# Keys of a decoder's two context attentions made per sequence, with a reordered head and filler matmuls

## What is computed

```
x = x + _L0_attn_ref(_layernorm(x, axis=-1), ...)   # 16 heads of 8, adds its own input
x = x + _L0_xattn_ref(_layernorm(x, axis=-1), ctx_768, ...)   # 8 heads of 64 over the context
x = x + _L0_ffn_ref(_layernorm(x, axis=-1), ...)    # "mixer": 16 heads of 8, tokens in two classes
x = x + _L1_attn_ref(_layernorm(x, axis=-1), ...)   # delta rule, a scan over the tokens
x = x + _L1_xattn_ref(_layernorm(x, axis=-1), ctx_768, ...)   # 16 heads of 64 over the context
x = x + _L1_ffn_ref(_layernorm(x, axis=-1), ...)    # ternary weights, gelu
```

```
k = encoder_hidden_states @ Wk
scores = jnp.einsum('bhsd,bhkd->bhsk', q, k) * scale
```

## Time and profile before

| | |
|---|---|
| median of 3 runs | 436.03 us (434.42 to 437.32) |
| the profiled execution | 432.25 us |
| its span, first to last instruction | 430.5 us |
| granted TensorE clock, mean over the span | 0.988 |
| TensorE busy (matmul) | 358.3 us, 83% |
| VectorE busy | 267.5 us, 62% |
| ScalarE busy | 209.8 us, 49% |
| POOL busy | 120.7 us, 28% |

### The profile page before, as it was taken

The page is one execution under the profiler, slowest core; times in us unless marked ns, Lnnn a source line. Parts: engine busy times, 40 slices in busy tenths (PEclk is TensorE's granted clock), DMA queues, the critical chain, the costliest instruction groups (busy, mean ns, idle before and its releaser), DMA issues. The chain is left out here.

```text
span 430.5 us, 7408 instructions
## 1 busy us (share of the span) xinstructions
PE 358.3 (83%) x2801; PEld 206.1 (48%) x2801; DVE 267.5 (62%) x579; ACT 209.8 (49%) x359; POOL 120.7 (28%) x113
## 2 busy tenths in 40 slices
PE   2677788889888989768799998867978999999986
PEld 1444333345454644335455664533534556555555
DVE  4864654566646566567644677759886675667345
ACT  2354556546434453236566443524645664445534
POOL 4000000136454017000000231114694655356500
PEclk9998999999999999899999998999999999999999
DMA  7700000010000000000001000000000000000000
GB/s 200 204 1 2 0 2 1 2 50 2 0 2 2 0 0 2 0 0 3 3 2 50 0 2 0 2 0 0 2 2 2 2 0 2 2 0 2 2 2 24
DMA packets 9688, 6.16 MB, mean 14 GB/s; under 512 B 3755, under 2 KB 8758, under 8 KB 9654
## 3 DMA queue, kind: packets, MB, share of 16 engines
q1 hardware_dynamic: 9654, 5.69, 5.1%
HBM read 5.39 MB, written 0.26 MB: 13 GB/s over the span
## 5 line engine op out<-in xcount | busy, mean ns | idle before, releaser
L1269 DVE TENSOR_REDUCE mxw<-PS 128x2 f32<-128x1024 f32 x48 | 58.5, 1222 | 23.8 <-PE PS L637 23.4
L1040 ACT ACTIVATE Pc<-PS 128x1024 f32<-128x1024 f32 x48 | 49.1, 1023 | 22.3 <-PE PS L665 21.1
L552 POOL TENSOR_TENSOR Psum<-Pc 128x512 f32<-128x512 f32 x24 | 31.0, 1293 | 100.5 <-ACT Pc L1040 99.8
L1266 DVE TENSOR_REDUCE mx<-PS 128x4 f32<-128x1024 f32 x32 | 39.0, 1223 | 24.2 <-PE PS L630 24.1
L693 PE MATMUL ACC<-Pc,V 128*64 128x256 f32 x384 | 52.0, 391 | 0.0
L554 POOL TENSOR_TENSOR Psum<-Psum,Pc 128x512 f32<-128x512 f32 x22 | 27.9, 1269 | 38.3 <-ACT Pc L1040 38.0
L1040 ACT ACTIVATE Ps<-PS 128x1024 f32<-128x1024 f32 x32 | 32.7, 1023 | 12.0 <-PE PS L649 10.9
L693 PEld LDWEIGHTS ACC<-Pc,V 128*64 128x64 f32 x384 | 23.4, 136 | 23.6 <-issue 15.2
L705 PE MATMUL PS<-ones_h 128*128 128x512 f16 x102 | 25.4, 391 | 4.7 <-DVE small_kv L1318 2.5
L555 POOL TENSOR_TENSOR Psum<-Psum,Pc 128x512 f32<-128x512 f32 x22 | 28.0, 1273 | 1.7
L658 PE MATMUL PS<-Qhl,Khl_a 64*128 64x256 f16 x384 | 26.5, 271 | 0.9 <-DVE scratch L1438 0.5
(11 more groups left out here) (290 smaller groups left out, 701.7 us busy)
## 6 DMA issues: line engine op xcount, KB each, us to landing
Qm<-mrow SPq DMA_DIRECT2D x64, 0.5 KB, 1.7
wq_c<-in_c_Wq_dram SPq DMA_DIRECT2D x1, 512.0 KB, 5.5
spread<-in_c_Wo_dram SPq DMA_DIRECT2D x1, 512.0 KB
Pc<-in_ctx_dram SPq DMA_DIRECT2D x1, 384.0 KB, 4.6
wk_c<-in_c_Wk_dram SPq DMA_DIRECT2D x1, 384.0 KB, 6.7
wv_c<-in_c_Wv_dram SPq DMA_DIRECT2D x1, 384.0 KB, 7.6
csth<-in_const_dram SPq DMA_DIRECT2D x1, 320.0 KB, 4.9
x<-in_x_dram SPq DMA_DIRECT2D x2, 128.0 KB, 2.2
```

The lines of the kernel that those rows point to most:

```text
L552: alone(v.tensor_tensor(t, p[:, :, 0, :], p[:, :, 1, :], ALU.add), "sums_done")
L1040: e = A(to, src.rearrange("p a c -> p (a c)"), ACT.Exp, scale=PHASES[name].scale)
L1266: last = v.tensor_reduce(to, src.rearrange("p e (t s) -> p e t s", t=2), AX, ALU.max)
L1269: last = v.tensor_reduce(to, src, AX, ALU.max)
```

## The change

Four things are done.

1. Keys per sequence: K and K2 exist now for b = 0 and b = 1, each with one f32 matmul of 512 columns, one area, copies of 128x512. The plan places 24 pairs of jobs instead of 12; in the first attentions at steps 2 to 8 and 12 instead of 3, 6, 8 and 12. K moves from the kinds that take two areas to those that take one, which also moves the areas of all jobs behind it until the ring meets again.
2. Head: sequence 1's ln stands behind sequence 0's ln2 and xt.
3. POOL writes ones_h before everything else, and 12 filler matmuls stand ahead of the first transposes.
4. prep does its four matmuls with high halves first and waits for the low half only then.

```diff
-    K0, K1 = ([[job("K", n, 0, u), job("K2", n, 0, u)] for u in range(PHASES[n].U)] for n in (x0, y1))
+    (K0, K0_), (K1, K1_) = ([[[job("K", n, b, u), job("K2", n, b, u)] for u in range(PHASES[n].U)] for b in range(B)]
+                            for n in (x0, y1))
...
-    head = ln + ln_ + ln2 + xt + [job("kq", a0, 0)]
+    head = ln + ln2 + xt + ln_ + [job("kq", a0, 0)]
...
-        3: K0[0], 6: K0[1], 8: K0[2], 10: [zT], 11: [out] + ln + V0[0], 12: ln2 + V0[1] + K0[3], 13: xt + V0[2],
+        2: K0[0], 3: K0_[0], 4: K0[1], 5: K0_[1], 6: K0[2], 7: K0_[2], 8: K0[3], 10: [zT], 11: [out] + ln + V0[0], 12: ln2 + V0[1] + K0_[3], 13: xt + V0[2],
...
-        -8: V1[4], -7: K1[1], -5: K1[2], -3: K1[3], 1: [qx], 3: [rs], 7: [rt], 10: [rv], 11: [zT, qx_], 12: [out, rs_] + ln, 13: ln2 + V1[5], 14: xt,
+        -8: V1[4], -7: K1[1], -6: K1_[1], -5: K1[2], -4: K1_[2], -3: K1[3], -2: K1_[3], 1: [qx], 3: [rs], 7: [rt], 10: [rv], 11: [zT, qx_], 12: [out, rs_] + ln, 13: ln2 + V1[5], 14: xt,
...
-        -8: [dg_], -5: K1[7] + [dt], -4: [s0], -2: [s1], 0: [s2], 2: [s3], 4: [oT], 5: [dl], 6: [dl2],
+        -8: [dg_], -6: K1[7], -5: K1_[7] + [dt], -4: [s0], -2: [s1], 0: [s2], 2: [s3], 4: [oT], 5: [dl], 6: [dl2],
...
 WARM = {
+    job("xt"): 12,
...
-    BANKS = {k: n for n, ks in ((2, ("prep", "M", "S", "ctx", "K", "V", "dp", "dt", "sp")),
-                                (1, ("xt", "kq", "vs", "turn", "Q", "zT", "out", "most", "qt", "simT", "qx", "rs", "rt", "rv", "dg", "oT",
+    BANKS = {k: n for n, ks in ((2, ("prep", "M", "S", "ctx", "V", "dp", "dt", "sp")),
+                                (1, ("xt", "kq", "vs", "turn", "K", "Q", "zT", "out", "most", "qt", "simT", "qx", "rs", "rt", "rv", "dg", "oT",
...
-                    after(sp, "K", "cross0", 0, 3)
+                    for k in range(B):
+                        after(sp, "K", "cross0", k, 3)
...
+            alone(v.memset(ones_h[:], 1.0), "warm_set")
             alone(v.memset(spread[:], 0.0), "pool_set")
...
-            alone(v.memset(ones_h[:], 1.0), "ones_set")
...
-                    after(pe, "kq", name, b)
+                    pe.wait_ge(sem("kq_high"), count("kq", name, b))
...
-                    for X, w in enumerate((spread_k, spread_q)):
-                        for uu in range(2):
-                            to, unit = dst[:, X, uu * S:(uu + 1) * S], slice((2 * u + uu) * P, (2 * u + uu + 1) * P)
-                            mm(to, w["h"][:, unit], hl16[:, b, 0, X * S:(X + 1) * S], start=(uu == 0), stop=False)
-                            last = mm(to, w["l"][:, unit], hl16[:, b, 1, X * S:(X + 1) * S], start=False, stop=not classes and uu == 1)
+                    for part, half in enumerate("hl"):
+                        if half == "l":
+                            after(pe, "kq", name, b)
+                        for X, w in enumerate((spread_k, spread_q)):
+                            for uu in range(2):
+                                to, unit = dst[:, X, uu * S:(uu + 1) * S], slice((2 * u + uu) * P, (2 * u + uu + 1) * P)
+                                last = mm(to, w[half][:, unit], hl16[:, b, part, X * S:(X + 1) * S], start=(part == 0 and uu == 0),
+                                          stop=part == 1 and not classes and uu == 1)
...
-                    for h in range(B):
-                        last = mm(dst[:, h, :], wk2[name][:, u * P:(u + 1) * P], ctxT[:, h * SC:(h + 1) * SC],
-                                  start=True, stop=True)
-                    last.then_inc(sem("ring"), 1)
+                    mm(dst[:, 0, :], wk2[name][:, u * P:(u + 1) * P], ctxT[:, b * SC:(b + 1) * SC],
+                       start=True, stop=True).then_inc(sem("ring"), 1)
...
-                    A(keys(name, 0, u), src.rearrange("p a c -> p (a c)"), ACT.Identity).then_inc(sem("k_high"), 1)
+                    A(keys(name, 0, u)[:, b * SC:(b + 1) * SC], src[:, 0, :], ACT.Identity).then_inc(sem("k_high"), 1)
...
-                    v.tensor_tensor(keys(name, 1, u), src.rearrange("p a c -> p (a c)"), keys(name, 0, u), ALU.subtract)\
+                    t = slice(b * SC, (b + 1) * SC)
+                    v.tensor_tensor(keys(name, 1, u)[:, t], src[:, 0, :], keys(name, 0, u)[:, t], ALU.subtract)\
```

More of the change, by code:

```diff
@@ L189, in schedule @@
     qt, kq, sim, simT, vs = mixer_front(1)[3:]
-    classes = V1[0] + cross_tail(x0, 1) + ln + [job("gsum")] + V1[1] + V1[2] + ln2 + xt + [qt, sim, kq, vs, job("tg")] + K1[0] + [simT, job("cls", f0)] + V1[3] + tern
+    classes = V1[0] + cross_tail(x0, 1) + ln + [job("gsum")] + V1[1] + V1[2] + ln2 + xt + [qt, sim, kq, vs, job("tg")] + K1[0] + K1_[0] + [simT, job("cls", f0)] + V1[3] + tern
     two = attentions((f0, 0, -9, 0), (f0, 1, -4, 0))
@@ L200, in schedule @@
     place_in(two, {
-        -8: V1[4], -7: K1[1], -5: K1[2], -3: K1[3], 1: [qx], 3: [rs], 7: [rt], 10: [rv], 11: [zT, qx_], 12: [out, rs_] + ln, 13: ln2 + V1[5], 14: xt,
+        -8: V1[4], -7: K1[1], -6: K1_[1], -5: K1[2], -4: K1_[2], -3: K1[3], -2: K1_[3], 1: [qx], 3: [rs], 7: [rt], 10: [rv], 11: [zT, qx_], 12: [out, rs_] + ln, 13: ln2 + V1[5], 14: xt,
         15: [dp, rt_], 16: [dn, dn2, dg], 18: [dt]})
-    ends = [rv_, s0] + V1[6] + [zT_, s1, out_] + V1[7] + [s2] + ln_ + [s3] + K1[4] + [oT] + ln2_ + [dl] + xt_ + K1[5][:1] \
-        + [dl2, yT, dp_] + K1[5][1:] + [dout] + ln4 + K1[6][:1] + ln24 + xt4 + [dn_] + K1[6][1:] + [dn2_]
+    ends = [rv_, s0] + V1[6] + [zT_, s1, out_] + V1[7] + [s2] + ln_ + [s3] + K1[4] + K1_[4] + [oT] + ln2_ + [dl] + xt_ + K1[5][:1] + K1_[5][:1] \
+        + [dl2, yT, dp_] + K1[5][1:] + K1_[5][1:] + [dout] + ln4 + K1[6][:1] + K1_[6][:1] + ln24 + xt4 + [dn_] + K1[6][1:] + K1_[6][1:] + [dn2_]
     three = attentions((y1, 0, -9, 0), (y1, 1, 13, 2))
@@ L624, in maxima @@
                         after(pe, "Q", name, b, u // 2)
-                        after(pe, "K", name, 0, u)
+                        after(pe, "K", name, b, u)
                 dst = take(j)
@@ L700, in keep_busy @@
                 if not warm_ready:
-                    pe.wait_ge(sem("ones_set"), 3)
+                    pe.wait_ge(sem("warm_set"), 1)
                     warm_ready.append(True)
@@ L715, in _ @@
                     if j == first_cross_s:
-                        pe.wait_ge(sem("ones_set"), 3)
+                        pe.wait_ge(sem("ones_set"), 2)
                         pe.wait_ge(sem("one_row_set"), 3)
```

## The result

The changed kernel takes 419.62 us (median of 4 runs, 418.54 to 419.66), beside it the kernel before 435.23 (median of 4, 431.81 to 437.32); ratio 0.964, 95% interval 0.958 to 0.971. Forecast were 424.6, between 419 and 432, with a chance of 0.85 for faster by over 1%. The profiled execution takes 419.58 us, span 417.8: 12.7 less than that of before (432.25), where the sum of the prediction had 11.4.

A forecast was written before the change was run, and what follows sets the result against it. TensorE, busy 83% of the span and mostly waiting for PSUM areas, was the bound. 2.8 + 2.6 + 4.2 + 2.2 - 0.4 = 11.4 us off 432.25 left 420.9; plus 3.8, median 424.6, range 419 to 432.

The forecast's parts named there:

- Head: Kernel start up to ScalarE's copy at 13.13 us: earlier rows, full clock and split spreading gain 2.8 us (0.3 to 3.5).
- First attentions: 30 to 75 us: sum of waits stays, clock's 1.6 us and a 0.99 us wait are gained; 2.6 us.
- Mixer's units: 157 to 190 us: waits of 2.45 and 2.01 shrink to 1.2 and 0.8, clock held; 4.2 us (0.5 to 6).
- Delta rule: 255 to 290 us: fillers need only sequence 0's low half, now before the reduction; 2.2 us (1.0 to 2.7).
- Costs: Extra copy time on VectorE and ScalarE, 3.8 us of engine time, charged at 0.4 us, at most 3.8.
- ring of areas: Six areas taken in other positions, 30 to 185 us; TensorE waits there for reductions, not areas: zero, plus or minus 1.5.
- slower: Rival: 16 halves ahead of the delta rule each stall TensorE 1.9 us; with 13 stalls 442.3 us; chance 0.06.
- step to the median: Whole kernel: 3.8 us, old median 436.03 above its profiled execution, added to the predicted 420.9 us.
- waits whole: Rival: each low half queues behind a reduction, so only head and delta rule gain, 5.0 us: 431.0; chance 0.18.
- Clock not held: Rival: pauses behind the head's transposes and keys, and the 1.9 us wait, lower the clock: 427.9 us; chance 0.11.
- Fillers too long: Rival in the head: TensorE starts at 2.2 us, fillers end at 7.3, gain 1.0 less: 425.6; no separate chance.
- signs: Trace marks of being right: copy about 10.3, spreading rows at most 0.3, clock 1.00 at 30-62 us, line 1324 waits at most 2.

The follow-up runs named there:

- head_only: Changed kernel with whole key units in two areas back at their old places, the new head kept; 431.36 us.
- keys_only: Changed kernel with its head put back (old norm order, no 12 fillers, ones and spreading as before), split keys kept; 423.02 us.
- turn_fillers: Changed kernel with 5 more filler matmuls of 512 columns ahead of the second turn of the first attention; 420.48 us.
- low_half_first: Changed kernel with each low half put ahead of the reductions of its step on VectorE; 422.59 us.
- u7_late: Changed kernel with both halves of the last key unit at the place of the whole one; 423.18 us.
- cross0_whole: Changed kernel with the keys of the first cross attention alone whole again, in two areas at their old places; 425.83 us.
- two_areas: Changed kernel, same order on every engine, but each half unit of keys takes two PSUM areas; 439.78 us.
- no_fillers: Changed kernel without the 12 filler matmuls ahead of the first transposes; 420.99 us.

## Why the prediction was right, and where it was not

- Head, 2.8 forecast: 2.98 at ScalarE's copy, 3.1 at the full clock (head_only, keys_only). Start of the fillers 0.98 for 1.2, their end 6.08 for 6.2, spacing 0.43 as read. The normed rows stand at 5.22 + 0.62 = 5.84 for 5.8, so the lower gain of 2.6, reckoned from the Trainium skill's rule on POOL and VectorE (GPSIMD Engine Reference, section 1 Specifications), did not come. The reading behind it was weak: in the trace of before POOL's casts run from 3.65 to 5.14 us, beside the row of 0.17 as well as that of 0.47. By parts: fillers 1.8 (I had 1.25; the spreading's clock was missing), spreading 1.3 by its trace (I had 1.4).
- First attentions, 2.6 forecast: 2.8 in the traces, and by the path I gave: the waits keep their sum and the clock's 1.6 comes back. But the reason given for the clock, that after 1.9 us of waiting it stays, is refuted by turn_fillers. What holds is a frequency: over all executions the three kernels with whole keys in both attentions or with two areas have 0.965 to 0.988, the changed one 0.996 to 1.000. It is no sharp line: low_half_first and u7_late, with split keys in single areas, reach down to 0.984.
- Mixer's units, 4.2 forecast: 4.05 up to 181 us, and 0.7 more by the third turn, where a score matmul waits 0.23 us for ScalarE and not 0.75. The waits came about as laid out (1.2 and 0.8 forecast, 1.05 and 0.62 measured); the first even better than I wrote, for 1.22 + 0.68 - 0.86 is 1.04 and not 1.2. What I had not seen is that they hang on the ring's position, which the first attentions set (cross0_whole).
- Delta rule, 2.2 forecast: 2.3 in the wait (2.54 to 0.20); u7_late returns 1.8 of it in the wait. Another 1.1 us between 250 and 270 was low clock in the trace of before (four key matmuls 3.40 us there, 1.88 after), which my sum did not hold.
- Costs, 0.4: not separately visible. VectorE's busy sum rose by 1.1 us (267.5 to 268.6); no run tells how much of it is on the path.
- What failed in the sum's reasoning is the ring of areas, "zero, plus or minus 1.5", with the reason that TensorE waits there for reductions and not for areas. Two runs bear on it. cross0_whole shows what the position does: 3.9 us at the full clock where the first attentions' own waits were booked at 1.2, and 1.0 of it is one wait for an area that another job asks for. two_areas shows what the size does: 12.4 us at the full clock. My layout had the single areas in it, and so the waits came out right; but I priced as a side effect what the other terms stood on. The rival "slower" did not happen in the changed kernel (three waits over 1.3 us for a low half). In two_areas the kernel is slower than before, though with no wait for a low half over 2.0 us.
- The sum (11.4) was 1.3 short of the difference of the profiled executions (12.7), and that it was not further off is partly luck: 1.1 us that the head lost again at 19 us and 1.1 of low clock that went near the delta rule were both not in it, and cancel.
- The time itself, 424.6 for 419.6, missed by 5.0, and most of that, 3.8, came from the step to the median: I added the distance between before's median and its profiled execution to the changed kernel too. That distance was mostly low clock, of which before has more in many of its executions than in the profiled one (0.969 to 0.988, profiled 0.988). The changed kernel, at 0.996 to 1.000, does not have it.
- Of the rivals: waits whole, refuted (7.8 for 13.2 us). Clock not held: the low clock came, not behind the transposes and keys as the rival had it but at 19 us, and cost 1.1 us in the traced execution; two others have the same mean clock, the fourth has 1.000. Fillers too long, refuted.
- Of the signs, the copy (10.15 for 10.3), the clock from 30 to 62 us, the longest wait (1.74) and the fillers of the delta rule came as said. That no matmul of the spreading takes over 0.3 us holds in the head but not at 19.19 us, where eight take 1.69 us, 0.21 apart instead of 0.11.

## What to carry to other kernels

When jobs share a ring of buffers, count what each takes before counting when it is done: in this order of jobs, halving what the keys take was worth 12 us, and splitting them without that cost more than it gave. A part's price measured alone holds only as long as the ring stands in the same position behind it, so undo parts both singly and together. And before a profiled time is carried over to a median, look at the granted clock of all executions: a difference that is low clock in the one kernel need not be there in the other.

## What the runs showed of the chip that I had not expected

In these traces the granted clock falls behind pauses of 1.05 to 2.5 us (in cross0_whole once behind one of 0.65), but not behind the same pause each time: behind 1.69 us it stayed in the changed kernel and fell in turn_fillers, behind 2.12 us (ended at 252.72) and 1.05 us the same. Why it falls behind one and not the other stays open. With fillers in one pause (turn_fillers) the low stretches stood at later ones. With two of the pauses filled and others shortened, three of four executions ran at 1.000; no_fillers has two such, the changed kernel one, so four executions do not settle what the fillers did. Most of a kernel's scatter (before: 6 us, the changed one: 1.1) goes with this clock: after the correction the thirteen executions of before from which the slope was read lie within 429.0 to 429.6, the twenty others within 428.8 to 430.3.
